# One slot later: the low parts, the projection and the residual sum of a latent attention

## The reference, cut to what matters

```
q = (x @ wq)                      # 16 heads, 128 plain + 64 rotated columns
ckv, k_pe = x @ wkv_a             # 64 latent columns, 64 rotated columns
scores = q . k * scale, causal, softmax over the keys
out = attn @ v ; out @ wo         # v = ckv @ (value part of wkv_b)
x = x + result
```

## Time and profile before

| | |
|---|---|
| median of 3 runs | 940.77 us (940.66 to 945.98) |
| profiled execution | 944.91 us, of which span 942.9 us |
| busy share PE / DVE / ACT / POOL | 91% / 76% / 56% / 46% |
| second attention (its loop) | about 443 to 785 us of the span |
| granted TensorE clock there | 1.00 |

### The profile page before, as it was taken

How to read it: one execution, slowest core, us unless ns; L and a number is a source line. 1 busy time by engine, 2 the same in 40 slices (tenths; PEclk the granted TensorE clock), 3 DMA queues, 4 the chain that set the end, 5 groups by cost and what they waited for, 6 DMA issues and landing times.

```text
span 942.9 us, 19230 instructions
## 1 busy us (share of the span) xinstructions
PE 856.5 (91%) x6286; PEld 649.1 (69%) x6286; DVE 717.7 (76%) x2366; ACT 531.3 (56%) x1392; POOL 434.7 (46%) x683
## 2 busy tenths in 40 slices
PE   6678898889999999987999999999999997999996
PEld 5556666667765666655888787887888775666663
DVE  6567988889778887663968787787868686888872
ACT  5356544454354555545676676757586761555555
POOL 0348898887766665446202121221202012556655
PEclk9779999999999999989999999999999999999999
DMA  6333333332223557102112020202021022234331
GB/s 211 60 50 49 53 56 55 56 55 38 35 37 58 103 118 133 43 14 46 24 24 46 1 46 1 45 2 46 2 45 37 11 35 35 36 71 59 59 48 35
DMA packets 49938, 46.55 MB, mean 49 GB/s; under 512 B 5280, under 2 KB 47280, under 8 KB 49840
## 3 DMA queue, kind: packets, MB, share of 16 engines
q1 hardware_dynamic: 49840, 45.33, 26.2%
HBM read 11.40 MB, written 2.10 MB: 14 GB/s over the span
## 4 chain that ended last, share of the span: by engine, by line
PE 33%; DVE 15%; issue 3%; ACT 1%; POOL 1%; DMA 0%; POOLq 0%; SPq 0%; DVEq 0%; ACTq 0%
PE bank L301 8%; PE bank L1979 6%; PE bank L1987 4%; PE bank L1913 4%; DVE weights L1476 3%; PE bank L1928 3%; DVE weights L1466 3%; PE bank L1743 2%; PE bank L1756 2%; DVE q_lo L1456 1%; PE bank L1739 1%; DVE rope L1454 1%; PE bank L1782 1%; DVE xn L338 1%; DVE arena L1313 1%
## 5 line engine op out<-in xcount | busy, mean ns | idle before, releaser
L1313 DVE TENSOR_REDUCE arena<-bank 128x2 f32<-128x512 f32 (+1 forms) x192 | 130.9, 685 | 42.4 <-PE bank L1743 41.4
L924 ACT ACTIVATE weights<-bank 128x512 f32<-128x512 f32 x144 | 85.8, 596 | 109.1 <-PE bank L1756 108.3
L1006 ACT ACTIVATE weights<-weights,neg_max 128x128 f32<-128x128 f32 (+1 forms) x256 | 113.9, 449 | 39.2 <-DVE neg_max L1466 38.7
L727 POOL TENSOR_SCALAR_AFFINE_SELECT weights<-weights 128x256 f32<-128x256 f32 x144 | 68.6, 478 | 101.4 <-ACT weights L924 101.4
L1979 PE MATMUL bank<-kbT,arena 128*128 128x128 f32 (+1 forms) x512 | 105.1, 328 | 1.0 <-DVE y L447 0.9
L667 POOL TENSOR_SCALAR weights<-weights 128x512 f32<-128x512 f32 x64 | 97.6, 1537 | 12.5 <-ACT weights L832 12.5
L1743 PE MATMUL bank<-kf_stack,q_stack 96*128 96x256 f32 (+1 forms) x256 | 99.7, 432 | 0.0
L1013 ACT ACTIVATE weights<-bank 128x384 f32<-128x384 f32 x128 | 62.7, 490 | 61.0 <-PE bank L1987 60.5
L1466 DVE CUSTOM_DVE_ANT_0 weights<-bank,arena 128x128 f32<-128x128 f32 (+1 forms) x256 | 80.2, 350 | 14.6 <-PE bank L1979 12.6
L301 PE MATMUL bank<-x_hi,wb_hi 128*128 128x256 f32 x256 | 83.8, 327 | 2.8 <-DVE q_lo L1456 2.8
L1476 DVE TENSOR_SCALAR weights<-weights,inv_sum 128x128 f32<-128x128 f32 (+1 forms) x256 | 81.3, 360 | 4.6
(11 more groups left out here) (236 smaller groups left out, 2514.2 us busy)
## 6 DMA issues: line engine op xcount, KB each, us to landing
q_stack<-q_hi SPq DMA_DIRECT2D x96, 128.0 KB, 4.5
arena<-arena SPq DMA_DIRECT2D x64, 128.0 KB, 2.5
q_stack<-q_lo SPq DMA_DIRECT2D x48, 128.0 KB, 5.3
ka_stack<-k_hi SPq DMA_DIRECT2D x32, 76.5 KB, 2.8
x_all<-x SPq DMA_DIRECT2D x8, 256.0 KB, 5.1
st_wo<-b_wo SPq DMA_DIRECT2D x8, 256.0 KB, 4.2
arena<-b_wqn SPq DMA_DIRECT2D x8, 256.0 KB, 3.3
out<-x_all SPq DMA_DIRECT2D x8, 256.0 KB, 2.1
```

The source lines that it names most:

```text
L924: a.activation(s["pT"][(STEPS * b + k) % N_PT], p2[k % 2][:, :], ACT.Exp).then_inc(s["exp"], 1)
L1006: last = a.activation(p, p, ACT.Exp, scale=-1.0, bias=neg_max[:, h % 4, t:t + 1], accum_out=sums[:, h % 4, t:t + 1])
L1313: v.tensor_reduce(into, p1[k % 2][:, :].rearrange("p (s g k) -> p s g k", s=n, g=NC), AX.X, ALU.max, negate=True).then_inc(s["maxed"], 1)
```

## The change

Three steps move by one slot. On VectorE the subtraction for the low part moves from slots 1, 5, 9, 13 to slots 2, 6, 10, 14, and the residual sum from slot 3 to slot 4. On TensorE the projection moves from slots 2, 6, 10, 14 to slots 3, 7, 11, 15. Nothing is added or removed, ScalarE, GpSimd and SP keep their programs, and what follows the loop stays as it is.

```
@@ VectorE @@
-                    if h == 1 and b > 0:
+                    if h == 2 and b > 0:
                         low_oT(b - 1, QUADS - 1)
-                    elif h % 4 == 1 and h > 1:
+                    elif h % 4 == 2 and h > 2:
                         low_oT(b, h // 4 - 1)
-                    if h == 3 and b > 0:
+                    if h == 4 and b > 0:
                         residual_b(b - 1)
@@ TensorE @@
                     if h % 4 == 0:
                         after_quad(b, h // 4 - 1, attend_b)
-                    elif h % 4 == 2:
+                    elif h % 4 == 3:
                         after_quad(b, h // 4 - 1, project_b)
                     turn_probs(b, h)
```

## The result

The changed kernel takes **957.36 us** (median of 4 runs, 955.11 to 959.26) against 940.97 (4 runs, 940.66 to 945.98). The ratio on record is 1.0155, 95% interval 1.0131 to 1.0179. The kernel is slower, as forecast. The forecast was 11.0 us; the medians lie 16.4 apart, the ratio stands for 14.6 (0.0155 of 940.97), and the spans of the two profiled executions, 957.2 and 942.9, lie 14.3 apart.

What follows compares the result with a forecast made beforehand. TensorE was taken as the bound (42.35 of 43.0 us busy per batch). Six steady batches at 1.6 (9.6), 0.5 in batch 0 and 0.9 in the last gave 11.0 us: 940.8 to 951.8, range 943.5 to 957.

Steps and rivals of the forecast that it cites:

- The loop of 3.25: A turn two slots behind a quad's slot cannot start before that slot's turn + 3.25 us, through ScalarE and VectorE.
- The three turns that had to wait: Turns 14, 2 and 6 on TensorE: each waits about 1 us, with VectorE's weights as releaser.
- Slots 14 and 15: Without the projection TensorE idles 1.22 before turn 14; next scores at 701.20 instead of 700.94, a loss of 0.3 us.
- Slots 0 to 3: Latent projection ends 0.44 early, but the projection now follows it in slot 3; TensorE's scores of slot 4 1.2 late.
- Slots 8 to 13: Second attention, steady batch: nothing lost, since the absorbed queries give TensorE 4.8 us between turns 8 and 10.
- Slots 3 to 7: VectorE enters slot 5 1.4 us late; turn 7 and the scores of slot 8 come 1.6 late.
- The two normalizations: VectorE, slots 5 and 6: one 0.48 shorter, the other 0.48 longer beside GpSimd; 1.6 stays, with only one 1.1 or 2.1.
- The last batch: Turn 7 at 759.76 against 758.88, 0.9 us lost; its other quads have feed-forward steps beside them.
- Batch 0: No quad in slots 0 to 3, leaving slots 6, 7, 14 and 15: an estimated loss of 0.5 us.
- the waits only change place: Rival, 0.18: VectorE's 3.8 us are slack, TensorE fills the gaps, only slots 14 and 15 lose: about 942.6.
- The faster case: Rival, 0.07: projection never waits for the low part, turns 7 and 15 meet finished probabilities: 933.3.
- The worse one: Rival, 0.07: each delay slows the next stage, slot 10 loses like slot 14; 1.6 + 1.2 a batch, 958 to 960.

## Why the prediction came out as it did

**Direction and mechanism were right.** The loop of 3.25 was measured at 3.27, twice. The three turns that had to wait are the three that wait; the wait of VectorE before the first rotary products, forecast near 1.9, is 1.79; the wait for the rounded sum is gone. That the loop is what turns 14 and 2 wait for is shown by moving ScalarE's rounding out of it, which shortened it by the rounding's time, and, for turn 14, by another piece of work in slot 14, which ended its wait. Turn 6 is another matter: it waits for VectorE's row of work from 633.04 on, and the kernel that moves its quad alone loses 0.71 with the same wait. That the projection had been the cover of this row follows from the order of the work; no other cover was tried there.

**Slots 14 and 15:** forecast 0.3, measured 0.31 in the changed kernel and alone. **Slots 0 to 3:** the scores of slot 4 forecast 1.2 late, measured 1.18. **Slots 8 to 13:** forecast nothing, measured 0.00 alone and no loss between slot 8 and slot 12.

**Slots 3 to 7: the term that was mis-sized.** The forecast had the scores of slot 8 1.6 late; they are 1.89 late. Two steps were off, both by reading a distance from start to start where another engine waits for an end. First, the latent projection's end: I added 0.39, a distance from start to start in the timeline, to durations that run to an end. In the chain the three transposes of a turn that waited take 0.55 (at 626.63), so the end of the latent projection lies 12.72 behind the scores of slot 14, not 12.55, and VectorE's rotary products start at 16.61, not 16.40. TensorE's next scores are not hurt by this, their starts being counted from starts; VectorE is, because it waits for an end. Second, from the start of slot 6 (638.68) to turn 6 VectorE takes 1.74, where 1.13 and 0.48 were 1.61. The 1.13 ran to VectorE's own next instruction, at 669.12, and a turn waits for the end of the multiplications. The trace of before shows the gap: 0.80 from a reciprocal to its turn, but 0.66 from this one to 669.12:

```profile
668.46 0.16 DVE L1473 RECIPROCAL inv_sum<-sums 128x2 f32<-128x2 f32 x1
```

The two make 0.34 of the 0.38 by which turn 6 is later than forecast (23.99 behind the scores of slot 14, against 23.61). By the end of the batch 0.26 of it was left: a period of 44.84, not 44.6, and 1.6 us over the six batches.

**The two normalizations** moved as forecast: slot 5 fell from 1.03 to 0.58 and slot 6 rose to 1.02, so the two shifts cancel, and neither the 1.1 nor the 2.1 was right but the value between. With the residual sum put back, slot 5 returned to 1.03. The Trainium skill, SBUF — State Buffer, section on who interferes with whom, says that GpSimd and a two-port VectorE operation hold one shared port pair in turn; the runs agree, with 0.43 to 0.48 us more for the pair of multiplications that stands beside a GpSimd instruction of 0.73 to 0.76. Normalization 6 ends at 640.38, 0.16 behind the end of that instruction.

**The last batch** was forecast at 0.9 and took 2.8. The 0.9 came true as a delay and not as a loss: turn 4 is 0.58 late and turn 7 is 1.46 late, 0.88 between them, but turn 13 is only 0.40 late (34.95 behind the scores of slot 14 of batch 6, where it was 34.55), so most of that delay, and of the 0.58 that came in from slots 14 to 0, is made up again by then. What the forecast lacked altogether is the end: from turn 13 to turn 15 the changed kernel takes 6.82 (785.88 to 792.70) where before took 4.92 (774.03 to 778.95). Turn 14 waits 1.73 where turn 15 had waited 1.20, and the projection behind it runs 1.30 longer at half the clock. From turn 15 to the last residual sum another 0.5 is lost, the first part of it still at that clock: 0.40, 1.90 and 0.5 are the 2.8. "Its other quads have feed-forward steps beside them" is the step that failed: true of the quad of slot 8, false of the last. Batch 0 lost 0.7 instead of 0.5.

**Against the range.** The measured median lies 0.36 above the range's top; by the ratio of 1.0155 it would be 955.4 on the forecast's 940.8, inside it. Of the 5.4 us by which the 16.4 between the medians exceed the forecast's 11.0, 3.3 are in the trace: 1.6 in the steady batches, 1.9 in the last, 0.2 in batch 0, less 0.4 at the start of the loop. The other 2.1 lie in the executions: before's profiled one stood 3.9 above its median, after's stands 1.9 above.

**The rivals.** That the waits only change place (942.6) is ruled out by the quads of slots 2 and 6, which lose 0.87 and 0.71 alone. The faster case needed the exponentials to end earlier, and rows of after show them where the earlier trace rows had them. The worse one (958 to 960) came near the measured time, but not by its mechanism: slot 10 lost nothing.

## What to carry to other kernels

Before moving a piece of independent work on an in-order engine, ask which loop through the other engines it stands beside, and write down that loop's length from rows; the piece is its cover, and the price is the loop less what is left in its place, less what was being lost there already (an idle time of 1.08 cost 0.31 behind slot 12). Two steps that belong together (a subtraction and the product that reads it) cost more apart than together: 8.0 us a batch for the subtraction without the product, 2.6 for the product without the subtraction, the residual sum moved with either, and 1.9 for all three. Count to an end where another engine waits for an end, and from start to start only along one engine.

## What was not expected of the hardware

TensorE's clock fell behind two of the waits. In the last batch, TensorE was busy for 3.24 of 5 us with a wait of 1.73 at the end of it (785 to 790 and the row of turn 14); the granted clock was 1.00 there and 0.50 from 790.5 to 793.5, and twelve matmuls took 2.73 us instead of 1.43: about the factor of two between the levels of 1.2 and 2.4 GHz. With VectorE's moves alone, the projection behind the longest wait of a steady batch, 2.9, took 2.68, in a stretch at 0.72. The waits of 1.08, 0.64 and 1.01 in each steady batch of the changed kernel left it at 1.00, and so did 795 to 800, where TensorE was busy for only 3.22 of 5 us. What decides between these cases is not shown here.
